# First attention: splitting the score pair and reordering TensorE's work within a unit

## The chip, the cores and the metric

The kernel runs on one core of a Trainium2 chip. A time is the device time of one execution in microseconds (us); the metric is the median of several runs. The engines are TensorE (PE; its weight loads are PEld), VectorE (DVE), ScalarE (ACT), GpSimd (POOL) and SyncE (SP), which only issues transfers here. Each engine works through its own instructions in the order written, and they wait for each other through semaphores.

## The reference

Eight sequences of 512 tokens with 128 features go through two blocks of attention and routed experts. The change lies in the first attention, whose core is this, for 16 heads of 8 features:

```python
x_norm = layer_norm(x, g1, beta1)
q = apply_rope(x_norm @ Wq + bq) / sqrt(hd);  k = apply_rope(x_norm @ Wk + bk);  v = x_norm @ Wv + bv
scores = einsum('bhqd,bhkd->bhqk', q, k)
attn = softmax(scores)
out = einsum('bhqk,bhkd->bhqd', attn, v)
x = x + out @ Wo + bo
return x + relu(layer_norm(x, g2, beta2) @ W1 + b1) @ W2 + b2
```

Behind it each token is normalised, multiplied by a routing matrix, and sent to its best two of 16 experts. Then come a second attention and eight more experts; they are untouched.

## The kernel before, in words

`layer0_attention` treats one sequence (a batch `i` of 8) after the other. In a batch, heads go in four quads `g` of four heads, and a quad is cut into eight units `j` (`UQ`), so that a batch has 32 units, numbered `u = 8 g + j`.

Every head's scores are computed twice. The **logits** (`logits`, L1318: queries on the partitions, one 128x512 product each, two per unit) serve only to find each row's maximum: VectorE reduces each of them (`maximum`, L1124). They run ahead by four units and a quad, over three PSUM banks `FB`; a logit waits until the maximum of the logit three before it is taken. The **scores** (`scores`, L1359: keys on the partitions, two 128x512 products per unit, into the two halves of `ST`) already have the maximum subtracted; ScalarE takes the exponential of each (L1025) into `PT`. A score waits until the exponential of the unit before has read the same half of `ST`.

The **value products** (`values`, L1338) take the exponentials of a quad. They stand in units `j` 5 and 6 (first half of the quad) and in units 1 and 2 of the next quad (second half); ScalarE copies the finished bank `PV` (`copy_values`, L997) and TensorE turns it in unit 3 (`turn_values`, L1348), after which VectorE divides (`attend`). At `j` 5 TensorE turns a quad's maxima (`turn_max`, L1326), ScalarE copies them (`minus_max`, L992) and SP stores them into the rows of the queries (`stack_max`, L812), for which the first score of the next quad waits.

All else that TensorE does is cut into **pieces**, spread over the units by four tables (L669 to L673). All pieces share one PSUM bank, `PC`, so each piece waits (`front`) until ScalarE or VectorE has read the piece before it:

```python
EARLY = {26: [("turned", 0)], 28: [("projected", 0)], 31: [("projected", 1)]}
LATE = {0: [("projected", 2)], 3: [("projected", 3)], 12: [("v", 0)]}
TAIL = {7: [("at", 0)], 8: [("wo", 0)], 13: [("z", 0)], 15: [("hidden", 0)], 16: [("hidden", 1)],
        19: [("hidden", 2)], 20: [("hidden", 3)], 23: [("ffn", 0)], 24: [("ffn", 1)]}
ROUTE = {2: [("r_turned", 0)], 4: [("r_logits", 0)], 17: [("r_ranked", 0)]}
```

ScalarE's order in a unit (its `run`) is: both exponentials, then `minus_max` at `j` 5, then the copies of this unit's pieces (`evacuate`, L941 to L961; the router's is L383), then parts of the rotation (L982, L986), the normalisations (L214: `tail_scale` at unit 11, `scale` at 21 and 25) and `copy_values`. VectorE's order is: the unit's two maxima, then `part_max`, `residual`, measuring for the norms (L177, L182; units 9, 18, 23), the router's choice (`choose`, L439 to L473) in eight parts, and `route_measure` (L348) at unit 29 and `r.scale` (L368, L371) at units 31 and 1. GpSimd's order over a batch ends with: the norm's root (L189) after the measuring of unit 23, eight indirect writes of routed rows (`put_rows`, L489), then `add_up` (L872), for which `route_measure` waits, then the router's root (L357).

Of the kernel before, what the change touches and what calls it, by code (L numbers as in the profile page):

```python
# [14 lines left out]
P = 128  # L15
# [18 lines left out]
KR0 = STACK + 2  # L34
# [5 lines left out]
def sem(signal):  # L40
    return signal[0]


def per_turn(signal):
    return signal[1]


def turn(signal, i, n):

    return signal[0], i * signal[1] + (n + signal[2])  # L50
# [510 lines left out]
def layer0_attention(nc, ins, c, r, expert_w1, expert_w2):  # L561
# [5 lines left out]
    with ExitStack() as ctx:  # L567
# [5 lines left out]
        def sig(name, per=1, start=1):  # L573
            signals.append((r.ctx.enter_context(nc.semaphore(f"a_{name}")), per, start))
            return signals[-1]
# [6 lines left out]
        NQ = H // QUAD  # L582
        UQ = 2 * QUAD
# [19 lines left out]
        QS = w1_rows[0:KR0, 0:half_row].bitcast(BF16).rearrange("p (h s) -> p h s", h=H)  # L603
        KS = w1_rows[0:KR0, half_row:2 * half_row].bitcast(BF16).rearrange("p (h s) -> p h s", h=H)
# [27 lines left out]
        ST = ctx.enter_context(nc.psum_tensor("a_ST", [P, 2, S], F32))  # L632
# [26 lines left out]
        scored, exped = sig("scored", 2 * UNITS), sig("exped", 2 * UNITS, 2)  # L659
# [17 lines left out]
        def pieces(u, tail, n1, n2, routed):  # L677

            return ([(kind, -2, n) for kind, n in ROUTE.get(u, []) if routed]
                    + [(kind, -1, n) for kind, n in TAIL.get(u, []) if tail]  # L680
                    + [(kind, 1, n) for kind, n in LATE.get(u, []) if n1]
                    + [(kind, 2, n) for kind, n in EARLY.get(u, []) if n2])
# [39 lines left out]
        def next_quad(i, g, k=1):  # L722

            return i + (g + k) // NQ, (g + k) % NQ

        def has_quad(g, k, n1):
            return n1 or g + k < NQ

        def ahead(i, g, u, n1):

            k, n = 1 + (u + AHEAD) // UQ, (u + AHEAD) % UQ
            if not has_quad(g, k, n1):
                return None
            b, q = next_quad(i, g, k)
            return b, [(UQ * q + n) * 2, (UQ * q + n) * 2 + 1]
# [494 lines left out]
        def _(pe):  # L1230
# [80 lines left out]
            def logits(i, n):  # L1311

                h, t = n // T, n % T
                if n % (QUAD * T) == 0:
                    g = h // QUAD
                    pe.wait_ge(*turn(stacked[g], i, per_turn(stacked[g])))
                pe.wait_ge(*turn(maxed, i, n - 2 if n >= BANKS else (0, -2, -1)[n]))
                pe.matmul(FB[n % BANKS][:, :], QS[0:STACK, h, t * P:(t + 1) * P], KS[0:STACK, h, :],  # L1318
                          start=True, stop=True).then_inc(sem(filled), 1)

            def turn_max(i, g):
                pe.wait_ge(*turn(mlow, i, g + 1))

                pe.wait_ge(*turn(attn, i, g - 1))
                for t in range(T):
                    last = pe.matmul(TB[0:2 * QUAD, t * P:(t + 1) * P], parted[:, t, :], identb[:, :],  # L1326
                                     start=True, stop=True)
                last.then_inc(sem(mturned), 1)

            def values(i, g, kt):  # L1330

                if kt % 2 == 0:
                    pe.wait_ge(*turn(exped, i, 2 * UQ * g + UQ * (kt // 2 + 1)))
                if kt == 0:
                    pe.wait_ge(*turn(vplaced, i, 1))
                    pe.wait_ge(*turn(pvcopied, i, g))
                for j in range(QUAD):
                    last = pe.matmul(PV[32 * j:32 * j + 32, :], V[:, kt, QUAD * g + j, :],  # L1338
                                     PT[:, QUAD * (kt // 2) + j, kt % 2, :], start=(kt == 0), stop=(kt == T - 1))
                if kt % 2:  # L1340
                    last.then_inc(sem(pv), 1)

            def turn_values(i, g):

                pe.wait_ge(*turn(pvcopied, i, g + 1))
                pe.wait_ge(*turn(attn, i, g))
                for t in range(T):
                    last = pe.transpose(TB[:, t * P:(t + 1) * P], pvs[:, t * P:(t + 1) * P], ident[:, :])  # L1348
                last.then_inc(sem(pvturned), 1)

            def scores(i, g, j):

                w, h = j // QUAD, QUAD * g + j % QUAD
                if j == 0:
                    pe.wait_ge(*turn(mstacked, i, 32 * (g + 1)))
                for kk in range(2):
                    kt = 2 * w + kk
                    pe.wait_ge(*turn(exped, i, 2 * (UQ * g + j) + kk - 1))
                    pe.matmul(ST[:, kk, :], KS[0:KR0, h, kt * P:(kt + 1) * P], QS[0:KR0, h, :],  # L1359
                              start=True, stop=True).then_inc(sem(scored), 1)  # L1360

            for use in FIRST + SECOND:
                piece(use, -1, opening, bank_of[use])
# [10 lines left out]
            def run(i, tail, n1, n2, routed, prev):  # L1374
                for g in range(NQ):
                    for j in range(UQ):
                        u = UQ * g + j
                        scores(i, g, j)
                        if j == 5 and has_quad(g, 1, n1):
                            turn_max(*next_quad(i, g))  # L1380
                        if ahead(i, g, j, n1):
                            b, ns = ahead(i, g, j, n1)
                            for n in ns:
                                logits(b, n)
                        if j in (1, 2):
                            if g:
                                values(i, g - 1, j + 1)
                            elif tail:
                                values(i - 1, NQ - 1, j + 1)
                        if j in (5, 6):  # L1390
                            values(i, g, j - 5)
                        for use in pieces(u, tail, n1, n2, routed):
                            piece(use, i, prev)
                        if j == 3:
                            if g:
                                turn_values(i, g - 1)
                            elif tail:
                                turn_values(i - 1, NQ - 1)

            turns(pe, run)  # L1400
            values(B - 1, NQ - 1, 2)
            values(B - 1, NQ - 1, 3)
# [1407 lines left out]
```

## Time and profile before

| | us |
|---|---|
| median of 3 runs | 1821.87 |
| lowest and highest | 1816.07, 1834.79 |
| span of the profiled execution | 1776.1 |
| TensorE busy | 1455.7 (82%) |
| VectorE busy | 1274.7 (72%) |
| ScalarE busy | 935.2 (53%) |
| GpSimd busy | 694.1 (39%) |

The span is from the first to the last instruction that the profiler saw; the 45.8 us between it and the median lie around it. The device time of the profiled execution itself is not among the times shown, so 1776.1 us is what it is known by. A TensorE record lasts from a product's start to its modelled end, and the next product starts long before that end, so a busy TensorE can still have room: the distance between starts is what counts.

### The profile page before, as it was taken

To read this page: it belongs to the slowest core of one execution; us is meant where nothing else is said; L and a number is where in the kernel's file an instruction comes from. 1 tells how busy PE (TensorE), PEld (TensorE's weight loads), DVE (VectorE), ACT (ScalarE), POOL (GpSimd) and SP (SyncE) were. 2 spreads that over 40 slices of the span, in tenths; PEclk is the share of its full clock that TensorE was granted. 3 is DMA by queue.
4 is the path that set the end of the run, shared out by engine and by line. 5 is a ranking of instruction groups with operands and counts; after the bars stand their busy time and mean duration, and the time that the engine had idled before them with its cause. 6 is when DMAs were issued, how large, how long until landed. Compare 5 with 4: busy or idle time off the path is not lost. (4 is left out here: it accounts for less than half of the span.)

```text
span 1776.1 us, 37567 instructions
## 1 busy us (share of the span) xinstructions
PE 1455.7 (82%) x11726; PEld 964.8 (54%) x11726; DVE 1274.7 (72%) x3482; ACT 935.2 (53%) x1914; POOL 694.1 (39%) x812
## 2 busy tenths in 40 slices
PE   3999999999999729995378887878888887837993
PEld 1224334333343319994256766666666665627993
DVE  6777888888787435555777879697978786834555
ACT  2577777777775505662435455454545453314561
POOL 3122342633520334554233344444444541233552
PEclk8699999999998969997689999898999998978997
DMA  6211111111110332222544443434344434132225
GB/s 158 66 42 59 47 52 53 61 53 49 49 62 15 128 123 67 73 72 82 164 150 126 126 128 106 131 109 129 112 125 122 130 111 138 38 130 56 71 72 162
DMA packets 122418, 166.37 MB, mean 94 GB/s; under 512 B 21490, under 2 KB 96018, under 8 KB 121586
## 3 DMA queue, kind: packets, MB, share of 16 engines
q1 hardware_dynamic: 113330, 145.69, 28.1%
q0 software_dynamic: 8896, 18.30, 3.0%
q8 instruction: 99, 1.62, 0.4%
q14 instruction: 93, 0.76, 0.1%
HBM read 116.04 MB, written 47.60 MB: 92 GB/s over the span
## 5 line engine op out<-in xcount | busy, mean ns | idle before, releaser
L1124 DVE TENSOR_REDUCE a_M<-a_F 128x1 f32<-128x512 f32 x512 | 325.8, 683 | 90.0 <-PE a_F L1318 88.1
L1025 ACT ACTIVATE L_W<-a_ST 128x512 f32<-128x512 f32 x512 | 276.8, 595 | 89.1 <-PE a_ST L1359 88.3
L2028 ACT ACTIVATE L_W<-c_ST 128x1024 f32<-128x1024 f32 x160 | 163.3, 1021 | 188.4 <-PE c_ST L2408 141.1
L2630 ACT ACTIVATE L_hT<-L_P,L_W1s 128x128 f32<-128x128 f32 x600 | 171.5, 368 | 142.9 <-PE L_P L2711 110.6
L2616 POOL DMA_INDIRECT L_yd<-L_ys,L_di x150 | 163.1, 1087 | 151.6 <-DVE L_ys L2662 147.2
L489 POOL DMA_INDIRECT L_xd<-L_XN,L_place_i x128 | 124.4, 972 | 146.5 <-issue 131.9
L1359 PE MATMUL a_ST<-L_W 74*128 74x512 bf16 x512 | 168.9, 395 | 11.1 <-ACT L_W L1025 6.3
L1318 PE MATMUL a_F<-L_W 72*128 72x512 bf16 x512 | 167.1, 403 | 7.7 <-DVE a_M L1124 6.9
L2702 PE MATMUL L_P<-L_xT,L_W1s 128*128 128x128 f32 x1200 | 161.0, 278 | 0.0
L2711 PE MATMUL L_P<-L_W,L_hT 128*128 x1200 | 159.1, 276 | 0.1
L2407 PE MATMUL c_ST<-ident,c_SD 128*128 128x128 f32 x512 | 149.7, 292 | 5.5 <-ACT L_W L2028 5.5
L2702 PEld LDWEIGHTS L_P<-L_xT,L_W1s 128*128 128x128 f32 x1200 | 148.8, 195 | 0.0
L2642 DVE TENSOR_SCALAR L_W1s<-L_W 128x644 f32 x150 | 74.5, 497 | 102.2 <-DVE L_ys L2662 69.8
L2711 PEld LDWEIGHTS L_P<-L_W,L_hT 128*128 128x128 f32 x1200 | 146.3, 192 | 0.4 <-issue 0.4
L1338 PE MATMUL a_PV<-L_W,a_V 128*32 128x512 f32 x1024 | 144.1, 637 | 1.0 <-ACT L_W L1025 1.0
L1359 PEld LDWEIGHTS a_ST<-L_W 74*128 74x128 bf16 x512 | 42.4, 98 | 157.0 <-ACT L_W L1025 124.2
L2381 PE MATMUL c_DIAG<-L_W,c_QS 72*128 72x128 bf16 x512 | 76.9, 227 | 48.5 <-DVE c_SD L2155 48.5
L2408 PE MATMUL c_ST<-c_less,c_pick 128*128 128x128 bf16 x512 | 116.1, 227 | 0.0
L2142 DVE TENSOR_TENSOR c_inc<-c_INC,c_table 128x512 f32<-128x512 f32 x128 | 87.3, 682 | 32.7 <-PE c_INC L2376 32.0
L2414 PE MATMUL c_ST<-c_QS,L_W 126*128 126x384 bf16 (+2 forms) x384 | 110.1, 287 | 0.0
L2413 PE MATMUL c_ST<-c_less,c_pick 128*128 128x384 bf16 (+2 forms) x384 | 109.3, 285 | 0.0
L2376 PE MATMUL c_INC<-c_KI,c_QI 54*128 54x128 bf16 x512 | 51.2, 221 | 60.9 <-DMA c_QS<-c_rd 18.3
(430 smaller groups left out, 3164.9 us busy)
## 6 DMA issues: line engine op xcount, KB each, us to landing
c_QS<-c_q SPq DMA_DIRECT2D x32, 504.0 KB
c_QS<-c_rd SPq DMA_DIRECT2D x32, 378.0 KB
L_xg<-L_xd SPq DMA_DIRECT2D x150, 64.5 KB
L_W<-a_q SPq DMA_DIRECT2D x32, 288.0 KB
L_W<-a_k SPq DMA_DIRECT2D x96, 96.0 KB
L_W<-c_k SPq DMA_DIRECT2D x96, 96.0 KB
L_W<-in_L_w SPq DMA_DIRECT2D x8, 1024.0 KB
c_QI<-c_r SPq DMA_DIRECT2D x32, 216.0 KB
```

Source lines behind the costliest of these rows:

```text
L489: pool.indirect_dma_start(self.x_d, bass.IndirectOffsetOnAxis(self.place_i[:, i % self.NB, k, t:t + 1], 0), self.XN[:, i % self.NB, t, k, ...
L1025: act.activation(PT[:, j, kk, :], ST[:, kk, :], ACT.Exp).then_inc(sem(exped), 1)
L1124: dve.tensor_reduce(M[:, t, h:h + 1], FB[n % BANKS][:, :], AX_X, ALU.max).then_inc(sem(maxed), 1)
L1318: pe.matmul(FB[n % BANKS][:, :], QS[0:STACK, h, t * P:(t + 1) * P], KS[0:STACK, h, :], start=True, stop=True).then_inc(sem(filled), 1)
L1338: last = pe.matmul(PV[32 * j:32 * j + 32, :], V[:, kt, QUAD * g + j, :], PT[:, QUAD * (kt // 2) + j, kt % 2, :], start=(kt == 0), stop=(kt ...
L1359: pe.matmul(ST[:, kk, :], KS[0:KR0, h, kt * P:(kt + 1) * P], QS[0:KR0, h, :], start=True, stop=True).then_inc(sem(scored), 1)
L2028: act.activation(PT[:, j, :, :], ST[:, :, :], ACT.Exp).then_inc(sem(exped), 1)
L2407: pe.matmul(out, SD[:, g % 2, j, t, :], ident[:, :], start=True, stop=False, is_transpose=True)
L2616: pool.indirect_dma_start(y_d, bass.IndirectOffsetOnAxis(di[:, n % YB:n % YB + 1], 0), ys[:, n % YB, :], None).then_inc(scattered[n % YB], 16)
L2630: act.activation(hT[:, n % 2, f, :], PS[2 + 2 * (n % 2) + f // 2][:, (f % 2) * P:(f % 2 + 1) * P], func, bias=W1s[:, n % WB, F + f:F + f + ...
L2702: last = pe.matmul(PS[2 + 2 * (n % 2) + f // 2][:, (f % 2) * P:(f % 2 + 1) * P], W1s[:, n % WB, f * P:(f + 1) * P], xT[:, n % 3, :], start ...
L2711: last = pe.matmul(PS[6 + n % 2][:, 0:D], hT[:, n % 2, f, :], W2[:, bass.ds(e, 1), f, :].rearrange("p a d -> p (a d)"), start=(f == 0), st ...
```

## The change

`scores` now issues one of the two score products. TensorE's `run` orders a unit as: first score; then the value products if the unit has any, else the unit's pieces; second score; both logits; then `turn_max`, the pieces of a unit with value products, and `turn_values`. Before, it was: both scores, `turn_max`, both logits, value products, pieces, `turn_values`. No instruction is added or removed, and no other engine's program changes.

```diff
-            def scores(i, g, j):
+            def scores(i, g, j, kk):
 
                 w, h = j // QUAD, QUAD * g + j % QUAD
-                if j == 0:
+                if j == 0 and kk == 0:
                     pe.wait_ge(*turn(mstacked, i, 32 * (g + 1)))
-                for kk in range(2):
-                    kt = 2 * w + kk
-                    pe.wait_ge(*turn(exped, i, 2 * (UQ * g + j) + kk - 1))
-                    pe.matmul(ST[:, kk, :], KS[0:KR0, h, kt * P:(kt + 1) * P], QS[0:KR0, h, :],
-                              start=True, stop=True).then_inc(sem(scored), 1)
+                kt = 2 * w + kk
+                pe.wait_ge(*turn(exped, i, 2 * (UQ * g + j) + kk - 1))
+                pe.matmul(ST[:, kk, :], KS[0:KR0, h, kt * P:(kt + 1) * P], QS[0:KR0, h, :],
+                          start=True, stop=True).then_inc(sem(scored), 1)
...
                         u = UQ * g + j
-                        scores(i, g, j)
+                        b, ns = ahead(i, g, j, n1) or (i, [])
+                        uses = pieces(u, tail, n1, n2, routed)
+                        valued_here = j in (5, 6) or (j in (1, 2) and (g or tail))
+                        scores(i, g, j, 0)
+                        if j in (1, 2) and g:
+                            values(i, g - 1, j + 1)
+                        elif j in (1, 2) and tail:
+                            values(i - 1, NQ - 1, j + 1)
+                        elif j in (5, 6):
+                            values(i, g, j - 5)
+                        else:
+                            for use in uses:
+                                piece(use, i, prev)
+                        scores(i, g, j, 1)
+                        for n in ns:
+                            logits(b, n)
                         if j == 5 and has_quad(g, 1, n1):
                             turn_max(*next_quad(i, g))
-                        if ahead(i, g, j, n1):
-                            b, ns = ahead(i, g, j, n1)
-                            for n in ns:
-                                logits(b, n)
-                        if j in (1, 2):
-                            if g:
-                                values(i, g - 1, j + 1)
-                            elif tail:
-                                values(i - 1, NQ - 1, j + 1)
-                        if j in (5, 6):
-                            values(i, g, j - 5)
-                        for use in pieces(u, tail, n1, n2, routed):
-                            piece(use, i, prev)
+                        if valued_here:
+                            for use in uses:
+                                piece(use, i, prev)
                         if j == 3:
```

## Rows read from the trace of the kernel before

**Rows 1.** One line's answer for the scores, L1359, over the whole span.

```profile
L1359 PE MATMUL a_ST<-L_W x512: 376/381/634, 54.7 to 604.0; 74*128 74x512 bf16 x171
  DMA L_W<-a_less: 0.6, 1
```

**Rows 2.** Windows: stretch, busy time of each engine (instructions), clock granted, DMA share, GB/s.

```profile
38.00:55.00 17.00, 13.55 (x29) 2.81 (x30) 15.41 (x27) 0.82 (x2) 0.00 (x0) 0.58 0.72 134
...
330.00:400.00 70.00, 67.17 (x385) 27.21 (x384) 59.90 (x150) 52.76 (x104) 30.36 (x36) 1.00 0.18 55
```

**Rows 3.** Waits, 190 to 470 us (four batches): who waited for whom, sum, times, longest.

```profile
PEld a_ST L1359 <- ACT L_W L1025: 59.8, 108, 1.0
ACT L_W L1025 <- PE a_ST L1359: 36.9, 37, 2.6
```

**Rows 4.** Timeline, 341 to 344 us, unit 6 of batch 4: start, length, instruction, [idle before].

```profile
341.56 0.61 PE L1359 MATMUL a_ST<-L_W 74*128 74x512 bf16 x2
341.98 1.09 ACT L1025 ACTIVATE L_W<-a_ST 128x512 f32<-128x512 f32 x2 [1.11 <-PE a_ST L1359]
342.12 1.27 POOL L745 TENSOR_TENSOR a_rot<-a_rot 128x512 f32<-128x512 f32 x1
342.16 1.33 DVE L441 TENSOR_TENSOR L_work<-L_key,L_red 128x64 f32<-128x64 f32 x1
342.53 1.06 PE L1338 MATMUL a_PV<-L_W,a_V 128*32 128x512 f32 x8
343.52 0.60 PE L1359 MATMUL a_ST<-L_W 74*128 74x512 bf16 x2
```

**Rows 5.** Timeline, 360 to 364 us: units 15 and 16 and the start of 17.

```profile
360.17 0.61 PE L1359 MATMUL a_ST<-L_W 74*128 74x512 bf16 x2
360.58 0.22 DVE L432 TENSOR_TENSOR L_choice<-L_desc,L_red 128x64 f32<-128x64 f32 x1
361.05 1.02 PE L1297 MATMUL a_PC<-a_ZT,a_W 128*128 128x512 f32 x2
361.91 0.59 PE L1359 MATMUL a_ST<-L_W 74*128 74x512 bf16 x2
362.11 0.69 ACT L961 ACTIVATE a_hT<-a_PC,a_b1c 128x512 f32<-128x512 f32 x1 [0.42 <-PE a_PC L1297]
362.94 1.10 PE L1297 MATMUL a_PC<-a_ZT,a_W 128*128 128x512 f32 x2
363.88 0.60 PE L1359 MATMUL a_ST<-L_W 74*128 74x512 bf16 x2
```

**Rows 6.** Timeline, 344 to 346 us: the copy of unit 7's piece, in unit 8.

```profile
345.15 0.60 ACT L951 ACTIVATE a_ATT<-a_PC 128x512 f32<-128x512 f32 x1
```

**Rows 7.** Timeline, 372 to 377 us: ScalarE's extra work of unit 21, and unit 23's start.

```profile
374.28 1.63 ACT L214 ACTIVATE XN<-X,a_ns,rstd 128x128 f32<-128x128 f32 x4
...
375.81 2.14 ACT L1025 ACTIVATE L_W<-a_ST 128x512 f32<-128x512 f32 x4
...
376.44 0.87 PE L1359 MATMUL a_ST<-L_W 74*128 74x512 bf16 x2
376.91 0.10 PEld L1359 LDWEIGHTS a_ST<-L_W 74*128 74x128 bf16 x1 [0.38 <-ACT L_W L1025]
```

**Rows 8.** Timeline, 377 to 398 us: from unit 23 to the next batch.

```profile
377.58 1.95 PE L1304 MATMUL a_PC<-a_W,a_hT 128*128 128x128 f32 x16
...
377.96 1.29 DVE L1124 TENSOR_REDUCE a_M<-a_F 128x1 f32<-128x512 f32 x2
...
380.53 0.20 POOL L189 TENSOR_TENSOR ve<-mv,eps 128x4 f32<-128x4 f32 x1 [3.28 <-DVE mv L182]
...
392.83 1.29 POOL L872 TENSOR_TENSOR X<-X,a_XC 128x512 f32<-128x512 f32 x1
...
394.16 0.29 DVE L348 BATCH_NORM_STATS2 L_rstat<-X 128x6 f32<-128x128 f32 x1 [1.16 <-issue]
...
396.08 0.39 PE L1318 MATMUL a_F<-L_W 72*128 72x512 bf16 x1 [0.46 <-DVE a_M L1124]
```

## The prediction

> **What bounds the kernel now.** I read the lines first, for where the first attention lies: the scores' products run from 54.7 to 604.0 us [rows 1], so the change can touch 549 us of the span of 1776.1, or 68.7 us a batch. Then the windows: in a full batch of 70 us TensorE's records are busy for 67.17, VectorE's for 59.90, ScalarE's for 52.76 [rows 2]. The 67 is misleading: one score product lasts 0.38 us [rows 1] and two last 0.61 [rows 4], so starts lie 0.22 to 0.23 apart. The timeline, read by starts, gives TensorE's true idle time: in the four full batches, 190 to 470 us, I count about 6 us a batch in which it waits with nothing streaming. The waits show 59.8 us for scores that wait for an exponential [rows 3]; most of that is a weight load waiting behind running products, for TensorE's own idle time is far smaller. Nor is ScalarE saturated: it waits 36.9 us for scores [rows 3]. So TensorE is the bound in most units and hands over to ScalarE or VectorE for parts of a microsecond in some. The gain cannot exceed 6 us a batch; whatever the new order delays by more than the slack beside it is lost.
>
> **A unit with value products (16 of 32).** Unit 6 lasts 1.96 us [rows 4]: scores at 0, logits behind them, value products at 0.97, next score at 1.96. An exponential starts 0.42 after its score; two take 1.09 together and one 0.60, so they follow at 0.49. New order: first score 0, value products 0.31, second score 1.30, logits 1.52 and 1.74, next unit 1.96. Every product takes what it took, and the length is the same: no term. But the second exponential moves from 0.91 to 1.72. Behind the pair ScalarE had 0.97 us free before the next exponential (from 1.41 to 2.38) and now has 0.17; the 0.8 us that it gains lies between its two exponentials, where its order has no work. Everything ScalarE does besides stands behind the second one. That is the cost of the change.
>
> **Neighbouring pieces: +1.95 us a batch.** Pieces share the bank PC. Units 15 and 16 [rows 5]: the piece starts at 361.05 and takes 0.86 to the next score; its copy starts at 362.11, lasts 0.69, and the next piece starts at 362.94, 0.15 to 0.25 later than without a wait. New, counted from unit 15's start: piece 0.22 to 1.08, second score 1.08, its exponential 1.51, copy 2.0 to 2.7; TensorE has finished its logits and unit 16's first score by 1.95 and waits until 2.74. The two units, 3.71 now (360.17 to 363.88), take 4.25: +0.55. Units 7 and 8: the copy [rows 6] starts 0.22 after unit 8's start now and 0.97 in the new order, where the second piece could start at 0.22 but waits to 0.98, against a wait of 0.17 for a score there now: +0.6. Units 2 and 3 alike: +0.5. Units 19 and 20 have a transposition between: +0.2. Units 3 and 4: +0.1. Units 31 and 0 are covered by the wait of the last step. Bounds of the sum: 1.0 to 2.5.
>
> **ScalarE's long extras: +1.15.** In unit 21 it copies maxima and normalises, 1.63 us [rows 7], then does four exponentials without a break (2.14). With the second exponential 0.5 later and the turned maxima behind the logits, the normalising starts 0.75 later against the unit; unit 22's first exponential ends at 2.77 of the unit where TensorE is ready at 1.96: +0.8. The normalising behind unit 11 takes as long (it waits for a chain that starts at unit 8's piece, 0.4 later): +0.35. Bounds: 0.3 to 1.7.
>
> **Waits that go: -0.8.** Two scores in a row take 0.87 instead of 0.60 where the second waits for its exponential [rows 7]; in four or five units of a full batch. Now other products stand between them. In units 5, 13 and 23 the whole 0.26 goes. Bounds: 0.5 to 1.3.
>
> **The chain over GpSimd: +1.2.** The expert piece of units 23 and 24 takes 1.95 us, some 1.7 between starts [rows 8], and now stands before the unit's logits. The first maximum of unit 23 moves from 1.52 to 2.58 after the unit's start; VectorE measures for the norm behind it, so GpSimd's root (380.53) moves by 1.3 to 1.4 against unit 24. From there GpSimd needs 13.6 us to VectorE's 394.16, and VectorE already makes TensorE wait (396.08) [rows 8], so nothing covers it. Given back: unit 31's piece is finished while TensorE waits. Then unit 2's routed piece waits for VectorE's scaling, which keeps its distance from 394.16. Net +1.2, bounds 0 and 1.6.
>
> **SP's and the router's terms: nothing.** The maxima turned at unit 5 of a quad come 0.9 us later to SP's two stores, and the next quad's first score needs them three units on; only one such wait was seen, 0.6 us [rows 1], and I see at least 1.9 us of slack left of it in full batches. The router's subtraction (L441) takes 1.33 us where the same shape takes 0.22 [rows 4, 5]; it ends with GpSimd's addition (342.12 + 1.27 = 343.39). It will start about 1 us later, so I count it as ending where it ends now, bound to GpSimd. If its 1.33 were its own, unit 7 would grow by 0.6 us, 4 us in the kernel: that is in my range. The Trainium skill (SBUF — State Buffer, "Who interferes with whom") says that a VectorE instruction with two SBUF inputs is blocked while GpSimd reads SBUF; by that rule the sum stays as it is, and by the duration alone it would be 4 us higher.
>
> **Sum.** 1.95 + 1.15 - 0.8 + 1.2 = 3.5 us in a full batch. Batches 2 to 5 are full: 14. Batches 1 and 6 lack the router or the next norm, 2 each; 0 and 7 lack more, 1 each. Together +20 us: span 1776.1 to 1796. The median of the runs lies 45.8 above the profiled span, all of it outside what changes: 1821.9 + 20 = 1842.
>
> **Rivals.** A measurement of this kernel can tell about 1%, 18 us, from no change.
> (a) *Faster.* The scores' waits are the real loss, and ScalarE's late second exponential costs nothing since its 53% leave room. Then the 0.26 us go in five units, and half of the other scores' waits, together 2.5 us a batch, and the added terms stay near 0: about -18, 1804. The point that decides is ScalarE's free 0.97 us: if its extras mostly fit into the 0.17 that is left plus one unit's reserve. For it: most value units give ScalarE nothing to copy. Against it: the copies of rows 5 and 6 have their reader right behind them. Chance 0.12.
> (b) *Even.* The same terms, but the GpSimd chain has slack that I don't see, and the neighbouring pieces cost their lower bound: 1.0 + 0.7 - 1.2 + 0 = 0.5 a batch, some +4: 1826. Chance 0.25.
> (c) *Much slower.* Delays add up: the subtraction's time is its own, and all terms take their upper bounds, 2.5 + 1.7 - 0.5 + 1.6 + 0.6 = 5.9 a batch, +35: 1857. A clock that falls would add to it: before the first scores, where TensorE waited for data, the granted clock was 0.58, half the time at 1.2 GHz, against 1.00 in the full batch [rows 2]; I see no wait over 1.5 us in the new order, and give it no price in the sum. The Trainium skill (TensorE: Matmul & The Clock Gate, "The HAM clock gate") says that activity holds the clock up and idleness lets it fall; by that rule a tenth of the stage at the lower level would cost up to 55 us. Chance 0.1.
>
> **How the numbers follow.** My forecast, 1842, has 0.53, with its own range 1832 to 1854. The line of 1% slower, 1840, runs through it: 0.33 of the 0.53 lie above, and with (c) slower has 0.43. Faster by 1%, under 1804, is half of (a) and a little more, 0.08. The rest, 0.49, is within 1%. The range leaves out the outer half of (a) and of (c): 1808 to 1860.
>
> **What would show it.** Right: in full batches 73 to 74 us between equal units instead of 70; pieces in units 16, 8 and 3 starting 0.7 us behind a ready TensorE; unit 22 near 2.8 us; GpSimd's root 2.5 us after unit 24's start; value units still 1.96. The first score pair's 0.87 rows are gone. Wrong: if second exponentials are late but the copies' readers aren't, (a) or (b) holds; if unit 31's logits come no later against unit 24, the chain's term is 0.

## The result: slower by 2 per cent, and a profile after that differs by more

The kernel after takes 1858.8 us, the median of 4 runs (1854.04 to 1864.18), against 1821.8 us before (1816.07 to 1834.79, 4 runs): a ratio of 1.021 (1.016 to 1.025). I had forecast 1842 and a range of 1808 to 1860. Here and below, ratios leave out runs more than 1.5% above the fastest of their kernel, while medians are of all runs.

The profiled execution of after has a span of 1862.6 us, in a run timed at 1864.18. So only 1.6 us lie around this span. The 45.8 us that I put there for before are not there either, if its span lies as close to its time: the execution of before that I read was then some 44 us faster than its timed ones. The two profiles must not be subtracted as they stand. First the scores' line over the whole span, as in [rows 1]:

```profile
L1358 PE MATMUL a_ST<-L_W x512: 376/382/634, 56.9 to 675.0; 74*128 74x512 bf16 x171
...
  DMA L_W<-a_less: 7.5, 11
```

The first attention now takes 618 us from its first score to its last, against 549: 69 us, where the timed runs differ by 37. Another 15.5 us of the two spans' difference lie behind the last score, where nothing was changed (1187.6 against 1172.1). Windows of one batch and of a later one, columns as in [rows 2]:

```profile
190.00:260.00 70.00, 64.87 (x376) 25.87 (x374) 56.43 (x144) 51.23 (x98) 22.63 (x28) 1.00 0.15 47
...
330.00:400.00 70.00, 63.76 (x322) 23.43 (x321) 50.64 (x124) 45.40 (x86) 27.08 (x30) 0.88 0.17 54
```

Both have fewer of TensorE's instructions than the 385 of [rows 2], but the later one has also lost clock: 0.88. Much of this comes from a wait that was not in the trace of before at all. Timeline of after, from the second score of unit 29 of batch 3 to unit 31 (start, length, instruction, idle before):

```profile
341.64 0.39 PE L1358 MATMUL a_ST<-L_W 74*128 74x512 bf16 x1
...
341.87 0.60 PE L1318 MATMUL a_F<-L_W 72*128 72x512 bf16 x2
...
343.41 0.96 POOL L489 DMA_INDIRECT L_xd<-L_XN,L_place_i  x1 [0.31 <-issue]
344.39 1.27 POOL L872 TENSOR_TENSOR X<-X,a_XC 128x512 f32<-128x512 f32 x1
345.97 0.60 ACT L1025 ACTIVATE L_W<-a_ST 128x512 f32<-128x512 f32 x1 [4.21 <-remote]
346.01 1.29 DVE L1124 TENSOR_REDUCE a_M<-a_F 128x1 f32<-128x512 f32 x2 [4.40 <-remote]
...
346.62 0.61 PE L1358 MATMUL a_ST<-L_W 74*128 74x512 bf16 x1 [2.52 <-ACT L_W L1025]
...
347.88 0.63 PE L1358 MATMUL a_ST<-L_W 74*128 74x512 bf16 x1
```

The score of 341.64 normally has its exponential 0.42 later, at 342.06. It begins at 345.97. VectorE's maximum of the logit at 341.87 is late alike. TensorE stands idle for 2.52 us, and when it resumes one score lasts 0.61 to 0.63 us where it lasted 0.38. The granted clock there is 0.50, the lower of its two levels, 1.2 GHz instead of 2.4:

```profile
346.50:348.50 2.00, 1.88 (x5) 0.92 (x6) 1.96 (x13) 1.49 (x4) 0.00 (x0) 0.50 0.01 2
```

I call this a **late completion**. It is a finding of its own, taken up in the last section; the order's own cost has to be read from units that late completions don't touch.

**What the order does in such units.** Value units do as forecast. Timeline of after, unit 6 of batch 2, beside [rows 4]:

```profile
212.36 0.39 PE L1358 MATMUL a_ST<-L_W 74*128 74x512 bf16 x1
212.61 1.28 POOL L745 TENSOR_TENSOR a_rot<-a_rot 128x512 f32<-128x512 f32 x1
212.68 1.06 PE L1338 MATMUL a_PV<-L_W,a_V 128*32 128x512 f32 x8
213.64 0.33 DVE L441 TENSOR_TENSOR L_work<-L_key,L_red 128x64 f32<-128x64 f32 x1
213.67 0.39 PE L1358 MATMUL a_ST<-L_W 74*128 74x512 bf16 x1
213.90 0.60 PE L1318 MATMUL a_F<-L_W 72*128 72x512 bf16 x2
214.34 0.38 PE L1358 MATMUL a_ST<-L_W 74*128 74x512 bf16 x1
```

Value products at 0.32, second score at 1.31, next unit at 1.98, against 0.31, 1.30 and 1.96 forecast. Pieces that stand in neighbouring units do as forecast too. Units 15 and 16, beside [rows 5]:

```profile
232.03 0.38 PE L1358 MATMUL a_ST<-L_W 74*128 74x512 bf16 x1
232.25 1.02 PE L1297 MATMUL a_PC<-a_ZT,a_W 128*128 128x512 f32 x2
233.11 0.38 PE L1358 MATMUL a_ST<-L_W 74*128 74x512 bf16 x1
233.52 0.60 ACT L1025 ACTIVATE L_W<-a_ST 128x512 f32<-128x512 f32 x1 [0.48 <-PE a_ST L1358]
233.76 0.38 PE L1358 MATMUL a_ST<-L_W 74*128 74x512 bf16 x1
234.02 0.68 ACT L961 ACTIVATE a_hT<-a_PC,a_b1c 128x512 f32<-128x512 f32 x1
234.84 1.10 PE L1297 MATMUL a_PC<-a_ZT,a_W 128*128 128x512 f32 x2 [0.70 <-ACT a_hT L961]
```

The first piece ends at 232.25 + 1.02 = 233.27, but ScalarE waits until 233.52 for the second score, takes its exponential, and copies behind it. The second piece, ready behind the score of 233.76, starts 0.70 us late. Unit 8 shows the same, beside [rows 6], and one thing more, a wait of 0.65 us for SP's store of the maxima (`L_W<-a_less`) ahead of its first score:

```profile
215.96 0.10 PEld L1358 LDWEIGHTS a_ST<-L_W 74*128 74x128 bf16 x1 [0.65 <-DMA L_W<-a_less]
...
216.21 0.61 ACT L951 ACTIVATE a_ATT<-a_PC 128x512 f32<-128x512 f32 x1
...
216.97 1.13 PE L1273 MATMUL a_PC<-a_W,a_ATT 128*128 128x128 f32 x8 [0.60 <-ACT a_ATT L951]
```

And unit 22, beside [rows 7]:

```profile
247.54 0.59 ACT L992 ACTIVATE a_less<-a_TB 8x512 bf16<-8x512 f32 x1 [0.15 <-PE a_TB L1326]
...
248.03 1.63 ACT L214 ACTIVATE XN<-X,a_ns,rstd 128x128 f32<-128x128 f32 x4
...
249.57 1.65 ACT L1025 ACTIVATE L_W<-a_ST 128x512 f32<-128x512 f32 x3
...
250.19 0.10 PEld L1358 LDWEIGHTS a_ST<-L_W 74*128 74x128 bf16 x1 [1.11 <-ACT L_W L1025]
```

The chain of [rows 8] starts as forecast: unit 24's first score is at 252.86 and GpSimd's root at 255.47, 2.61 us behind it, where it was 1.17.

```profile
252.86 0.38 PE L1358 MATMUL a_ST<-L_W 74*128 74x512 bf16 x1
...
253.08 1.95 PE L1304 MATMUL a_PC<-a_W,a_hT 128*128 128x128 f32 x16
...
255.47 0.20 POOL L189 TENSOR_TENSOR ve<-mv,eps 128x4 f32<-128x4 f32 x1 [4.47 <-DVE mv L182]
```

### The profile page after: what moved, and what is told of

Read it like the earlier page. It is cut to its first block and busy times, and to the rows that moved or that the text cites. A ratio compares the mean times of both kernels' runs of the same rounds, so it can differ in the third digit from the quotient of the medians.

```text
span 1862.6 us, 37567 instructions
## 1 busy us (share of the span) xinstructions
PE 1498.2 (80%) x11726; PEld 973.7 (52%) x11726; DVE 1276.6 (69%) x3482; ACT 946.6 (51%) x1914; POOL 693.7 (37%) x812
## 5 line engine op out<-in xcount | busy, mean ns | idle before, releaser
L1025 ACT ACTIVATE L_W<-a_ST 128x512 f32<-128x512 f32 x512 | 297.0, 595 | 193.4 <-PE a_ST L1358 165.7
L1358 PE MATMUL a_ST<-L_W 74*128 74x512 bf16 x512 | 210.1, 417 | 35.3 <-ACT L_W L1025 30.1
L489 POOL DMA_INDIRECT L_xd<-L_XN,L_place_i x128 | 124.4, 972 | 150.4 <-issue 136.9
L1318 PE MATMUL a_F<-L_W 72*128 72x512 bf16 x512 | 175.1, 420 | 5.4 <-DVE a_M L1124 3.6
L1358 PEld LDWEIGHTS a_ST<-L_W 74*128 74x128 bf16 x512 | 51.6, 101 | 222.9 <-ACT L_W L1025 121.6
L1338 PE MATMUL a_PV<-L_W,a_V 128*32 128x512 f32 x1024 | 150.7, 664 | 0.7 <-ACT L_W L1025 0.7
L2159 DVE TENSOR_TENSOR c_SD<-c_DIAG,c_inc 128x512 f32<-128x512 f32 x128 | 87.0, 680 | 13.6 <-PE c_ST L2418 13.4
```

Source lines behind the costliest of these rows:

```text
L489: pool.indirect_dma_start(self.x_d, bass.IndirectOffsetOnAxis(self.place_i[:, i % self.NB, k, t:t + 1], 0), self.XN[:, i % self.NB, t, k, ...
L1025: act.activation(PT[:, j, kk, :], ST[:, kk, :], ACT.Exp).then_inc(sem(exped), 1)
```

## The experiments

Twelve more kernels ran, on three chips: the two kernels again and the two halves of the change on the first, ScalarE's order and the three kernels with GpSimd's writes halved or last on the second, the rest on the third. The kernel before took 1816.8 and 1817.7 us on the first two and 1775.4 (25 runs) on the third. Each ratio is to the runs of before on the same chip. **u3-23** and **u24-2** are the mean times from unit 3 to the start of 24 and from there to unit 3 of the next batch, in batches 2 to 5; the second stretch holds the late completions.

| kernel | median us | ratio to before (95%) | first to last score | u3-23 | u24-2 |
|---|---|---|---|---|---|
| before, profile shown ahead | | | 549.3 | 45.5 | 24.9 |
| after, first profile | 1858.8 | 1.021 (1.016 to 1.025) | 618.1 | 48.0 | 32.5 |
| before again | 1824.5 | 1.005 (1.001 to 1.008) | 576.2 | 45.2 | 27.4 |
| after again | 1865.1 | 1.029 (1.025 to 1.033) | 608.5 | 48.0 | 30.0 |
| values only | 1842.1 | 1.016 (1.012 to 1.020) | 594.6 | 47.2 | 28.0 |
| pieces only | 1852.8 | 1.020 (1.016 to 1.025) | 599.9 | 48.3 | 29.8 |
| ScalarE's order | 1838.7 | 1.013 (1.008 to 1.018) | 583.9 | 46.8 | 28.5 |
| after, writes halved | 1863.2 | 1.025 (1.021 to 1.029) | 606.4 | 48.4 | 31.5 |
| before, writes halved | 1841.6 | 1.011 (1.004 to 1.018) | 576.9 | 45.3 | 33.1 |
| before, writes last | 1875.4 | 1.029 (1.025 to 1.034) | 614.2 | 45.6 | 38.1 |
| before, writes spread | 1764.6 | 0.995 (0.991 to 0.9996) | 535.6 | 45.2 | 23.5 |
| after, writes spread | 1798.0 | 1.012 (1.004 to 1.020) | 562.1 | 48.0 | 24.7 |
| spread, ScalarE's order | 1771.7 | 0.997 (0.994 to 1.001) | 547.1 | 45.6 | 24.5 |
| expert pieces behind | 1799.4 | 1.011 (1.006 to 1.016) | 571.9 | 48.2 | 25.1 |

**Both kernels again**, unchanged.

> The kernel before, unchanged, for its trace: the first profile had a span of 1776 us where the timed runs took 1822. Theory A (the order of work costs): nothing in this kernel is late; the trace again shows units as before, about 70 us a full batch, and a time near 1822 whose excess lies in another stage. Theory B (in the changed kernel, ScalarE and VectorE see TensorE's completions 1.5 to 5 us late once a batch while GpSimd writes routed rows, and TensorE's clock halves behind it): if this comes with the state of the chip rather than with the new order, this kernel shows it too when it takes 1822.

> The changed kernel, unchanged, on the same chip. Both theories: 1.015 to 1.025 of before. A: units 3 to 23 of a full batch 2.4 us longer than before. B: once a batch, near units 24 to 30, completions seen over 1.5 us late, in this trace too.

The unchanged kernel before comes out 0.5% above other runs of itself, so a difference of 0.5% says nothing in this study. Its profiled execution, at 1840 us the slowest of its ten, spent 576 us in the first attention where the profile ahead shows 549: it has late completions too, the longest in batches 6 and 7. Timeline of before again, units 28 and 29 of batch 3:

```profile
320.24 0.96 POOL L489 DMA_INDIRECT L_xd<-L_XN,L_place_i  x1 [0.30 <-issue]
...
321.04 0.26 DVE L1139 RECIPROCAL a_rec<-a_TB 128x16 f32<-128x16 f32 x1 [1.18 <-remote]
321.07 0.60 ACT L1025 ACTIVATE L_W<-a_ST 128x512 f32<-128x512 f32 x1 [1.33 <-PE a_ST L1359]
...
321.50 0.96 POOL L489 DMA_INDIRECT L_xd<-L_XN,L_place_i  x1 [0.30 <-issue]
...
322.45 0.60 ACT L1025 ACTIVATE L_W<-a_ST 128x512 f32<-128x512 f32 x1 [0.78 <-PE a_ST L1359]
322.49 1.37 DVE L1124 TENSOR_REDUCE a_M<-a_F 128x1 f32<-128x512 f32 x2 [0.87 <-remote]
```

So this loss belongs to the execution as much as to the order. u3-23 is what repeats: 45.2 and 45.5 before, 48.0 both times after.

**One half of the change each.** Values only: pieces stay behind the logits everywhere. Pieces only: value products and `turn_max` keep their places.

Values only, against after:

```diff
                         elif j in (5, 6):
                             values(i, g, j - 5)
-                        else:
-                            for use in uses:
-                                piece(use, i, prev)
                         scores(i, g, j, 1)
...
-                        if valued_here:
-                            for use in uses:
-                                piece(use, i, prev)
+                        for use in uses:
+                            piece(use, i, prev)
```

Pieces only, against after:

```diff
                         scores(i, g, j, 0)
+                        if not valued_here:
+                            for use in uses:
+                                piece(use, i, prev)
+                        scores(i, g, j, 1)
+                        if j == 5 and has_quad(g, 1, n1):
+                            turn_max(*next_quad(i, g))
+                        for n in ns:
+                            logits(b, n)
                         if j in (1, 2) and g:
                             values(i, g - 1, j + 1)
...
-                        else:
-                            for use in uses:
-                                piece(use, i, prev)
-                        scores(i, g, j, 1)
-                        for n in ns:
-                            logits(b, n)
-                        if j == 5 and has_quad(g, 1, n1):
-                            turn_max(*next_quad(i, g))
```

> Only the value products stand between the two scores; pieces follow the logits, as before. A: the waits between neighbouring pieces go (units 3, 8, 16, 20: together 2 us a batch less than the changed kernel), unit 22 stays near 2.76; total 1.005 of before. B: if the late completions need the expert piece ahead of the logits, they go and the ratio is about 1.00; if not, they stay and it is 1.01 or more.

> Only the pieces stand between the two scores of units without value products; value products follow the logits, as before. A: the waits between neighbouring pieces stay (+2 us a batch), unit 22 is 2.0 again; total 1.01 of before. B: late completions come or not with the place of the logits behind the expert piece; 1.02 if they come.

Unit by unit both halves did as expected (medians of batches 2 to 5). With values only, units 3, 8 and 16 take 2.35, 1.95 and 1.97 us, as before, and unit 22 takes 2.76, as in after. With pieces only it is the other way round: 2.90, 2.61, 2.67, and 1.97. The totals did not: 1.6% and 2.0% against 0.5% and 1% expected, and in u3-23 the halves cost 2.0 and 3.1 us against 2.8 for both. Each half brings waits that the whole doesn't have: with values only unit 20 takes 2.77 us against 2.23 in after, with pieces only units 9, 17, 21, 25 and 29 are 0.1 to 0.2 longer than there. Both traces also have late completions.

**ScalarE's order.** If the loss is that ScalarE waits for a late second exponential with its copies standing behind it, it must go when the copies stand ahead. The edit, shortened; the line in brackets names what else moves there:

```diff
                         for kk in range(2):
                             ...
                             act.activation(PT[:, j, kk, :], ST[:, kk, :], ACT.Exp).then_inc(sem(exped), 1)
+                            if kk == 0:
+                                if not valued_here:
+                                    for use in pieces(u, tail, n1, n2, routed):
+                                        evacuate(use, i)
+                                (tail_scale at u 11, scale at u 21 and 25, copy_values at j 2)
```

> The changed kernel, with ScalarE's order fitted to it: in units without value products it copies the pieces between its two exponentials, and there too it copies the values and does the normalisations of units 11, 21 and 25. Theory A (the second exponential comes late and ScalarE's copies stand behind it): units 3, 8, 16 and 20 get shorter by 0.5 to 0.7 us each and unit 22 returns to 2.0 to 2.3, about 3 us a batch and 20 us in all; ratio 1.01 or below. Theory B (late completions during GpSimd's writes make the excess): units as said, but the ratio falls by no more than the part of A, to 1.01 to 1.015. If neither order matters: 1.025 as the changed kernel.

A ratio of 1.013 against 1.021 and 1.029 for after on its own chips, and 1.2 us of the 2.8 in u3-23 are gone where some 3 us a batch were expected. Units 8, 16 and 22 are at 2.11, 1.97 and 1.98, but unit 12 has grown to 3.52 from 2.86: the normalisation of unit 11 now waits for GpSimd (L207) ahead of the second exponential, and holds it up.

**GpSimd's writes moved.** These three came from the late completions, which stand beside the eight indirect writes (L489). Halved: four writes, `add_up` and the root, four writes. Last: all eight behind the root.

```diff
                 if routed:
-                    r.put_rows(pool, i - 2)
+                    for n in range(CH * T // 2):
+                        r.put_row(pool, i - 2, n)
                 if tail:
                     ...
                     r.root(pool, i - 1)
+                if routed:
+                    for n in range(CH * T // 2, CH * T):
+                        r.put_row(pool, i - 2, n)
```

> The changed kernel with GpSimd's eight indirect writes of a batch in two halves: four, then add_up and the router's root, then four. Theory B (TensorE's completions are held up once several writes have followed each other, and the clock halves behind the pause): late completions go or shrink to under 1 us, 5 us a batch, 25 to 35 us in all; ratio about 1.005. If the number in a row does not matter: as many late completions, some 5 us later, ratio 1.02 to 1.03. A alone: 1 us a batch from the shorter chain, 1.02.

> The same move of four writes in the kernel before. B: the late completions of its units 28 to 30 go and the time falls by 20 to 35 us, ratio 0.98 to 0.985. A alone: 0.995 to 1.00, from the chain over GpSimd that is 5 us shorter but hardly binds here.

> The kernel before with all eight writes of a batch behind add_up and the router's root. B: the late completions move with the writes, by about 3 us or into the next batch, and stay as long, ratio 0.99 to 1.01; each ends where one of GpSimd's instructions ends. If they do not come from the writes, they stay in units 28 to 30.

None helps, and the gains expected with the writes halved did not come. There, batches 2 to 5 show no late completion in either kernel (batches 6 and 7 still have some); but VectorE's `r.scale` waits for the last write to land, and unit 1 grows to 7.5 us in after and to 9.4 in before, from about 2. With the writes last it takes 14.5, of which TensorE stands idle for 11.3. What is gained elsewhere is lost there. The late completions are also absent with all eight in a row behind the root, so a row of eight is not enough to make them.

**Writes spread.** To read the order by itself, the writes were laid where nobody waits: two ahead of the norm's root, three ahead of `add_up`, three behind it and ahead of the router's root. In before this also takes away the wait at the end of the chain of [rows 8]: units 31 and 1 are back at 1.74 and 1.96 us. The edit, shortened, the writes in brackets:

```diff
                     bias_tokens(i + 2)
+                (put_row n = 0, 1)
                     norm_root(pool, c, norm, i + 2, 1)
                     norm_shift(...)
-                    r.put_rows(pool, i - 2)
+                (put_row n = 2, 3, 4)
                     add_up(i - 1)
+                (put_row n = 5, 6, 7)
                     r.root(pool, i - 1)
```

> The kernel before with GpSimd's eight writes of a batch spread: two ahead of the second norm's root, three behind it, then add_up, three more, then the router's root; all are issued no later than before by more than 1.3 us. Theory B (TensorE's completions are held up after several writes in a row): no completion over 1 us late in batches 2 to 5, units 24 to 2 of a batch 24 to 25 us instead of 27.4, at most three writes follow each other; ratio 0.975 to 0.985. A alone: the router's root is reached earlier, 0.99 to 1.00. If the writes' landing binds as in the halved version: 1.01.

> The changed kernel with the same spread writes, to see the order alone, without late completions. A: units 3 to 23 still 48.0 us, units 24 to 2 about 26; against the spread kernel before that is 3.5 us a batch and 20 to 25 us in all, so a ratio of 0.99 to 1.00 against before. B with the order harmless: as fast as the spread kernel before, 0.98.

Timeline of GpSimd, before with the writes spread:

```profile
246.18 0.96 POOL L489 DMA_INDIRECT L_xd<-L_XN,L_place_i  x1 [0.30 <-issue]
247.16 1.27 POOL L872 TENSOR_TENSOR X<-X,a_XC 128x512 f32<-128x512 f32 x1
248.60 0.98 POOL L489 DMA_INDIRECT L_xd<-L_XN,L_place_i  x1 [0.17 <-issue]
...
254.29 0.20 POOL L357 TENSOR_TENSOR L_rve<-L_rmv,eps 128x4 f32<-128x4 f32 x1 [2.17 <-DVE L_rmv L352]
```

This is the clean pair: same chip, no late completion in either trace, and no timed run of the one (1757.5 to 1775.8, 10 runs) as slow as the fastest of the other (1790.5 to 1808.5, 4 runs). Windows of 190 to 470 us, first before spread, then after spread:

```profile
190.00:470.00 280.00, 273.10 (x1569) 111.24 (x1562) 235.79 (x600) 213.68 (x417) 122.96 (x142) 0.99 0.17 55
```

```profile
190.00:470.00 280.00, 258.25 (x1484) 103.90 (x1483) 226.79 (x568) 206.98 (x393) 113.31 (x133) 1.00 0.17 53
```

In the same 280 us the second does 5.4% fewer of TensorE's instructions (1484 against 1569) at nearly the same clock (1.00 against 0.99): it waits. Their scores, first and last, in the same order:

```profile
L1368 PE MATMUL a_ST<-L_W x512: 376/381/634, 55.3 to 590.9; 74*128 74x512 bf16 x171
```

```profile
L1367 PE MATMUL a_ST<-L_W x512: 376/382/635, 54.8 to 616.9; 74*128 74x512 bf16 x171
```

562.1 against 535.6: the order costs **26.5 us** of the first attention, 4.3 in each of batches 3 to 5 (72.7 against 68.4). In batch 2 it is 3.1, because before with the writes spread has a stretch at the lower clock level there, in units 5 and 6. The medians lie 33 us apart; the spans 32.2, of which 6.2 come behind the last score, where nothing was changed.

**ScalarE's order on the clean pair.** As above, but `tail_scale` and the `scale` of unit 25 keep their places behind the second exponential.

> The changed kernel with the spread writes and with ScalarE's copies between its exponentials (the normalisations of units 11 and 25 behind them again). A and B together: units 3 to 23 about 46.2 us, units 24 to 2 about 25.5, so within 0.5% of the spread kernel before; ratio 0.98 to 0.99. If the new order has a gain of its own once ScalarE follows it, it is faster than the spread kernel before.

Timeline, units 15 and 16, to be held against those of after above:

```profile
226.12 0.38 PE L1373 MATMUL a_ST<-L_W 74*128 74x512 bf16 x1
...
227.20 0.38 PE L1373 MATMUL a_ST<-L_W 74*128 74x512 bf16 x1
...
227.40 0.69 ACT L970 ACTIVATE a_hT<-a_PC,a_b1c 128x512 f32<-128x512 f32 x1 [0.26 <-PE a_PC L1312]
...
227.99 1.08 ACT L1035 ACTIVATE L_W<-a_ST 128x512 f32<-128x512 f32 x2
...
228.24 1.10 PE L1312 MATMUL a_PC<-a_ZT,a_W 128*128 128x512 f32 x2
```

The copy now starts 1.28 after the unit's first score instead of 1.99, TensorE is not idle ahead of the second piece, and unit 16 is back at 1.97 us. Unit 22 is at 1.98, u3-23 at 45.6 of 45.2 before and 48.0 after. This shows the main cause: TensorE's new order costs what it does largely because ScalarE's order was left as it was.

It does not give everything back. A batch of 3 to 5 takes 70.1 us, against 72.7 and 68.4: 2.6 of the 4.3 are gone. Unit 3 is still at 2.90, since unit 2 has value products and its piece is still copied behind the second exponential. Unit 1 takes 2.85 against 1.96: a logit there waits 0.71 us for a maximum of VectorE. The median falls by 26.3 us, from 1798.0 to 1771.7, but between the two traces the first attention falls by only 15.0; another 9.3 lie behind the last score, where nothing was changed. The kernel stays 7 us above before with the same writes, within the 0.5% expected; a gain of its own the new order does not show.

**Expert pieces behind the logits**, the unmoved writes, everything else as after: `valued_here` is also true in units 23 and 24, so that their pieces stand behind the logits.

```diff
-                        valued_here = j in (5, 6) or (j in (1, 2) and (g or tail))
+                        valued_here = j in (5, 6) or (j in (1, 2) and (g or tail)) or u in (23, 24)
...
-                        else:
+                        elif not valued_here:
```

> The changed kernel with the expert pieces of units 23 and 24 behind the logits again. A: GpSimd's root starts 1.2 us after unit 24's start instead of 2.6, and the cycle from unit 24 to unit 3 shrinks by about 1 us; ratio 1.015 to 1.02. B: late completions stay as they are. If the chain was mis-sized: no change, 1.025.

1799.4 (10 runs, 1784.5 to 1814.9) on the third chip, with no late completion in its trace. The root is at 1.16 behind unit 24, as expected. u24-2 is 25.1, 0.4 more than after with the writes spread: unit 1 takes 2.73 to 3.03 us against 2.18, waiting for the chain's end, and unit 2 is 0.2 shorter. So with the root where it was, the chain costs 0.4 in the new order; before it cost 1.4 (24.9 against 23.5). After itself was not run on that chip, so what its chain costs 1.4 us later has no undisturbed measurement.

## Why the prediction was right, and where its terms were off

**Direction and mechanism: right.** The cost lies where it was put: in copies and in the normalisation behind a late second exponential. Moving only ScalarE's work gives back 2.4 of the 2.8 us in u3-23. Of the signs that I had named, the equal units of a full batch take 72.7 us on the clean pair (73 to 74 forecast, but from 70 and not from 68.4), the pieces in units 16, 8 and 3 start 0.70, 0.60 and 0.47 late (0.7 forecast), unit 22 takes 2.76 (2.8), and value units 1.97 to 1.98 (1.96).

**The size: too small, and inside the range by luck.** 1858.8 is 1.2 us short of the range's end and outside the 1832 to 1854 that I gave my own mechanism. The timed difference is 37 us where I had 20; the order alone costs 26.5 in the clean pair's first attention. Run again on another chip, after took 1865.1 over a before of 1816.8. What lies on top there, late completions above all, was in no term.

**The terms**, in us a full batch, from the clean pair (the mean of batches 3 to 5, where the whole batch grew by 4.3; batch 2 is left out for the lower clock in it):

| step | forecast | measured |
|---|---|---|
| value units with nothing beside | 0 | 0 to 0.02 each |
| units 15/16 | +0.55 | +0.71, and 0.09 in unit 17 |
| units 7/8 | +0.6 | +0.65 in unit 8, +0.26 in unit 7 |
| units 2/3 | +0.5 | +0.56 |
| units 19/20, 3/4 | +0.2, +0.1 | +0.35, +0.11 |
| units 31/0 | 0 | +0.71 |
| units 1 and 2 | 0 | +0.22, +0.46 |
| ScalarE's extras, unit 22 | +0.8 | +0.76 |
| the same, unit 12 | +0.35 | 0, but +0.38 in unit 11 |
| waits that go | -0.8 | -1.07: units 5, 13, 23, 28 |
| chain over GpSimd | +1.2 | not in the pair |

The term that was mis-sized is *neighbouring pieces*: 1.95, bounds to 2.5, measured 3.4. Units 31/0 I had called covered by the chain's wait. In batch 1 of after, where no chain waits, unit 0 already takes 2.61 us against 1.90; the cover existed only where the chain ended late. And unit 7 grew because unit 8's first score waits 0.65 us for SP's store. *Waits that go* lies within its bounds. *ScalarE's extras* has its size, 1.14 of 1.15, but a third of it by luck: unit 12 did not grow. Unit 11 did, where a logit that waits for a maximum starts 1.13 us after the unit's start against 0.74. Units 1 and 2 were in no term: there a logit waits for a maximum, and a piece 0.30 us for VectorE's scaling (L371). Without the chain the steps sum to 2.3 and the pair shows 4.3; units 0 to 2 make 1.4 of the 2.0 between them, unit 7 0.3.

**Partial batches: wrong.** I gave batches 0, 1, 6 and 7 a cost of 1, 2, 2 and 1. The pair shows 0, 3.6, 4.1 and 2.7. In batches 1 and 6 pieces next to each other are there as in full ones (units 0, 8 and 16 grow by 0.6 to 0.7 in both), and I had scaled them down by what the batches lack without listing which pieces that is. Batches 0 and 7 can't be read that finely: both kernels run at the lower clock level for stretches in them, at different places. The four batches together make 4.4 of the 6.5 us between my 20 and the pair's 26.5; the full batches, 16.1 without a chain, are 2.1 above my 14 with one.

**The chain: its start right, its cost not shown.** The root moved to 2.61 behind unit 24 (2.5 forecast). The 1.2 us that this was to cost stays open. What arrives at the other end can't be read in after, since each full batch there has late completions in units 29 and 30.

**L441: right.** It now takes 0.33 us where it took 1.33. It starts at 213.64 and ends at 213.97; GpSimd's addition ends at 212.61 + 1.28 = 213.89. So all but 0.1 us of what it took beyond 0.22 was GpSimd's and not its own. The Trainium skill (SBUF — State Buffer, "Who interferes with whom") names one port pair shared by VectorE and GpSimd, held exclusively; by that rule the 1.33 goes when the overlap goes, and the trace agrees with its 0.33.

**SP's store: slightly wrong.** "Nothing" became 7.5 us in 11 waits against 0.6 in one; one of them is the 0.65 ahead of unit 8's score above, which comes back in the full batches. In the clean pair it is 6.2 against 1.8. I had claimed 1.9 us of slack and that was read from too few quads.

**The base: wrong, and harmless by luck.** I explained 45.8 us between profile and median as time around the span. It is 1.6 us in the profile of after. What the rest was, no trace of those timed executions shows. The trace of before again, 62 us longer than the one I read, has 27 of them in the first attention, with late completions, and 33 behind the last score. Had I taken it that the timed executions idle more, I would have asked whether waits at the lower clock level grow with the order too. The timed difference was 37 us in the result and 48 in both kernels again, against 33 in the clean pair.

**Rivals.** (a) and (b) are out: the readers of the copies were right behind them in every place named. (c) had the time, 1857 forecast, but not the mechanism: L441's second was not its own, and a full batch of the clean pair grew by 4.3 and not 5.9. Its sentence on a falling clock did come about, through waits of 2.5 us that I had said I did not see, though late completions made them: in after with the writes spread TensorE is never idle for more than 0.94 us in a full batch. I also misread the 0.58 there: between the levels 0.50 and 1.00 it means five sixths of the time at the lower one, not half. The Trainium skill (TensorE: Matmul & The Clock Gate, "The HAM clock gate") has idleness lower the clock; the trace of after agrees in that the 0.88 of 330 to 400 us goes with such a wait. Idle time of TensorE's records does not explain every fall: before with the writes spread is at 0.50 in unit 5 of batch 2, where eight value products take 1.93 us instead of 1.06, and TensorE's records show no idle time over 0.1 us in the batch so far.

```profile
199.59 1.93 PE L1347 MATMUL a_PV<-L_W,a_V 128*32 128x512 f32 x8
```

```profile
199.60:201.40 1.80, 1.80 (x9) 0.19 (x8) 1.73 (x5) 0.00 (x0) 1.72 (x2) 0.50 0.01 2
```

**A faster version?** Before with the writes spread has the lowest median of the study: 0.995 of before (0.991 to 0.9996), 1764.6 us against 1775.4 on the same chip. Units 31 and 1 no longer wait for the end of the chain, 1.2 us a full batch against the profile of before shown ahead (0.72 and 0.49). But before again differed from before by as much, so the gain is not shown. 0.995 is what theory A alone had expected; B's 0.975 to 0.985 could not come on a chip that shows no late completion. It was not tried on the slower chips. TensorE's new order with a matching ScalarE and the writes spread, 0.997 (0.994 to 1.001), is level with before and brings nothing.

## What to carry to other kernels

When one engine's order is changed, write down for each consumer where its instructions now stand between their inputs: a consumer in strict order that had its free time behind a pair of inputs loses it when the pair is pulled apart, even where the producer's own schedule grows by no more than 0.02 us a unit. Move the consumer's other work into the new gap in the same step, but not work that itself waits for another engine (unit 12 grew by 0.66 us that way), or leave the pair together. And before a profile serves as the base of a sum, compare its span with a timed run of the same execution: here only 1.6 us lay around a span, and tens of microseconds were a difference between executions.

## What was not expected of the hardware

**Completions seen late while GpSimd issues indirect writes.** In six profiles (after, both kernels again, both halves, and ScalarE's order on the second chip) ScalarE and VectorE saw results of TensorE 0.5 to 5 us late, one to five times a batch from batch 2 on, beside the eight writes of L489 and `add_up`. In the lines of before again the releases fall within 0.13 us of the ends of GpSimd's instructions: releases at 321.07 and 322.45, writes ending at 320.24 + 0.96 = 321.20 and at 321.50 + 0.96 = 322.46. In after, the release at 345.97 comes 0.31 after `add_up` ends at 344.39 + 1.27 = 345.66. Not every release is so near: in batch 7 one lies 1.9 us behind the last write in both kernels again. The later batches lose most: batch 7 takes 80.3 us in before again and 63.8 in before with the writes spread.

It is not the order alone, for before again has it. It is not eight writes in a row alone, for the first profile of before, before with the writes last and the kernel with the expert pieces behind have eight in a row and none of it. On the third chip none of four traces shows it, and before, timed there without a trace, took 42 us less (1775.4 against 1817). That points to the chip; but three of the four traces have the writes spread, after was not run there, and the cause was not settled.

**Untouched parts vary.** From the last score to the end, in code that no kernel changed, profiles took 1166.4 us (spread, ScalarE's order), 1172.1 (before, ahead), 1187.6 (after), 1205.2 (before again) and 1209.2 (before, writes last). Differences of a per cent between two profiles need not be the change's.
